# Attention stage of a token-merging block: raw-score search with three counts, dropped set added to transposed scores, values stationary in column groups

## What is computed

```python
qkv = (x_merge @ W_qkv).reshape(B, Mn, 3, NUM_HEADS, HEAD_DIM)
...
attn = jnp.einsum('bhqd,bhkd->bhqk', q, k) * SCALE
top_k = Mn // 8
kth = jax.lax.top_k(attn, top_k)[0][..., -1:]
attn = jnp.where(attn >= kth, attn, -jnp.inf)
attn = jax.nn.softmax(attn, axis=-1)
x_attn = jnp.einsum('bhqk,bhkd->bhqd', attn, v)
```

## Time and profile before

| | us |
|---|---|
| three runs: median (lowest to highest) | 15818.8 (15812.06 to 15821.48) |
| profiled execution, span | 16589.9 |
| attention in it, from its first score matmul to its last product | 3161 to 12898 |
| one step (one head), two consecutive ones | 72.85 and 71.58 |
| DVE / ACT / PE busy in 7000 to 7723 (10 steps) | 558.9 / 639.3 / 579.5 |

### The profile page before, as it was taken

One profiled execution on the slowest core, in us unless ns is written; L12 is line 12 of the kernel. 1 busy time (PEld: TensorE's weight loads), 2 busy tenths in 40 slices (PEclk: granted clock), 3 DMA queues, 4 the chain that ended last, 5 costly groups with the idle time before them and its releaser, 6 DMA issues. The chain is left out here.

```text
span 16589.9 us, 182616 instructions
## 1 busy us (share of the span) xinstructions
PE 10773.2 (65%) x53041; PEld 9450.6 (57%) x53041; DVE 10104.9 (61%) x21788; ACT 8925.2 (54%) x15905; POOL 2182.1 (13%) x2048
## 2 busy tenths in 40 slices
PE   4554776575888788878888866767678222229930
PEld 4454555375777777777777766767677222227720
DVE  7886344477777777777777777777777111111123
ACT  0000221486888888888888877878788010101100
POOL 2222111100000000000000000000000445440047
PEclk9999555555555555555555555555555555555555
DMA  2110000000000000000000000000000111111123
GB/s 71 37 31 22 19 21 19 16 5 4 6 6 6 6 6 6 5 5 6 6 6 6 6 4 5 5 6 6 4 6 4 30 34 30 34 26 32 32 47 58
DMA packets 624734, 282.98 MB, mean 17 GB/s; under 512 B 551011, under 2 KB 594595, under 8 KB 621061
## 3 DMA queue, kind: packets, MB, share of 16 engines
q1 hardware_dynamic: 563206, 222.50, 5.8%
q0 software_dynamic: 60928, 54.71, 1.6%
HBM read 167.59 MB, written 112.65 MB: 17 GB/s over the span
## 5 line engine op out<-in xcount | busy, mean ns | idle before, releaser
L971 PEld LDWEIGHTS a_psO<-a_v,a_pT 122*122 122x122 f32 x20736 | 4681.6, 329 | 0.0
L971 PE MATMUL a_psO<-a_v,a_pT 122*122 122x8 f32 x20736 | 4330.6, 333 | 0.0
L1047 ACT ACTIVATE a_signs<-a_e,a_te 122x1097 bf16<-122x1097 f32 x3456 | 4158.5, 1208 | 30.5
L961 PE MATMUL a_psT<-ident,a_p 122*122 122x122 f32 x10368 | 2918.3, 419 | 1789.9 <-ACT a_pT L1016 1342.0
L961 PEld LDWEIGHTS a_psT<-ident,a_p 122*122 122x122 f32 x10368 | 1955.5, 236 | 2138.9 <-issue 2138.7
L1016 ACT ACTIVATE a_pT<-a_psT 122x366 f32<-122x366 f32 x3456 | 1638.6, 474 | 388.7 <-PE a_psT L961 317.3
L1215 DVE TENSOR_REDUCE a_negmax<-a_psS 122x1 f32<-122x1097 f32 x1152 | 1493.7, 1297 | 572.7 <-PE a_psS L950 572.7
L1108 DVE SCALAR_TENSOR_TENSOR a_below<-a_e,a_te 122x1097 f32<-122x1097 f32 x1152 | 1553.0, 1348 | 210.7 <-remote 201.6
L1143 DVE SCALAR_TENSOR_TENSOR a_p<-a_e,a_theta 122x1098 f32<-122x1098 f32 x1152 | 1532.2, 1356 | 153.7 <-DVE a_flag L1184 135.0
L1054 ACT ACTIVATE a_e<-a_psS,a_negmax 122x1097 f32<-122x1097 f32 x1152 | 1384.5, 1202 | 290.9 <-DVE a_negmax L1215 290.8
L950 PE MATMUL a_psS<-a_k,a_q 72*122 72x512 bf16 (+1 forms) x3456 | 1325.7, 520 | 325.9 <-ACT a_e L1054 302.4
(11 more groups left out here) (343 smaller groups left out, 12886.9 us busy)
## 6 DMA issues: line engine op xcount, KB each, us to landing
r_bc<-pr SPq DMA_DIRECT2D x16, 1372.0 KB, 7.0
a_k<-kT SPq DMA_DIRECT2D x384, 51.5 KB
a_q<-qT SPq DMA_DIRECT2D x384, 51.5 KB
...
e_xg<-xbuf SPq DMA_DIRECT2D x160, 98.0 KB
ybuf<-e_yg SPq DMA_DIRECT2D x160, 98.0 KB
...
```

The source lines that it names most:

```text
L961: mm = pe.transpose(psT[:, j * QP:(j + 1) * QP], pr[t][:, kt * QP:(kt + 1) * QP], k.ident[0:QP, 0:QP])
L971: mm = pe.matmul(psO[:, 128 * u + t * HD:128 * u + (t + 1) * HD], pT[t % 2][:, kt, :], vh[u][:, kt * HD:(kt + 1) * HD], start=kt == 0, sto ...
L1047: act.activation(signs[t][:, :], ex[p][:, t, 0:MN], ACT.Sign, bias=te[p][:, t:t + 1], scale=-1.0, accum_out=sums[p][:, t:t + 1]).then_inc( ...
```

## The change

- **Scores stay raw.** DVE `evacuate` copies each score tile out of PSUM in two pieces (512 and 585 columns) with an accumulated maximum. `psS` is a single slot of 1536 columns; a piece is refilled as soon as it has been copied. There is no exp at this point.
- **Three counts.** ACT `count` counts at a first aim (mean + 1.185 deviations), at that moved by 0.9 of a slope step, and at that moved by another 0.5: 27 counts a head. The bracket and secant of `update` are gone; `move` is two small instructions, for tiles 0 to 4 and 5 to 8 apart.
- **Nearest 16.** DVE `window` writes min(score - te, sign) for the whole row, `nearest` takes the 8 largest of each of four quarters of it, `order` the 16 largest of these 32 (two MAX and a MATCH_REPLACE a tile). `search` picks the 137th; rows outside 16, or with more than 8 in a quarter, are marked, and marked tiles take the same kind of loop (`slow`) as before. The target count is 130 (TOPK - 7) instead of 133.
- **Dropped set.** `mask_tile` writes 1 where an element is under the threshold, as bf16 (`drops`), no accumulation. PE `fill` computes the transposed scores of 122 keys by 366 queries anew (`kt` stationary, `qt` moving, K = 74: two more rows carry minus the row maximum) and adds -32768 times the transposed `drops` in the same PSUM (three bf16 matmuls of 122 by 122, `drops` stationary). ACT `exponentials` then takes exp straight from PSUM for two blocks at a time (732 columns), 15 a head.
- **Values stationary.** PE `values`: v (122 by 32, with a column of ones for the row sum) is stationary, the 366 queries move (f32), and key block u writes to rows 32*(u mod 3) on of `psO`. ACT `take_out` copies 96 by 366 three times a head, and PE `turn_back` folds the three groups and turns the result back (9 f32 matmuls of 122 by 9). DVE `normalise` divides.
- **Row maximum.** PE turns it, DVE splits it into two bf16 parts (`split_peak`), SP writes it to DRAM and reads it back as two rows of `qt`. SP loads q and k twice a head (once for each orientation): 14 loads and a store in place of 7 loads.
- The pipeline is one step deeper (`old`: head s-3). A head's 15 slots are spread over 15 iterations of PE's step: iterations 0 to 9 belong to head s-2 (its slots 5 to 14), 10 to 14 to head s-1 (its slots 0 to 4).

In the diff, the removed functions are those printed above; lines that are only "..." stand for what is left out.

```diff
-AIM = TOPK - WIN // 2
-ROUNDS = 4
-Z_AIM = 1.15
+AIM = TOPK - 7
+Z_AIM = 1.185
...
-                                  SLOPE, None, ALU.mult).then_inc(free, 1)
+                                  -0.5 * SLOPE, None, ALU.mult).then_inc(free, 1)
...
+SUMK = PARTS * HP
+AUG = SUMK + 2
+CHUNKS = 3
+CT = QT // CHUNKS
+CW = CT * QP
+VC = 32
+NV = HD + 1
+PAIRS = [(0, 1), (2, 3), (4, 5), (6, 7), (8,)]
+PER = len(PAIRS)
+SLOTS = CHUNKS * PER
+RING = 3
+EDGES = [0, 275, 549, 823, MN]
+QUARTERS = len(EDGES) - 1
+HALF = 512
+FIRST_TILES = 5
+COUNTS = 3
+STEP = (0.9, 0.5)
+DROP = -32768.0
+LOWEST = -1.0e30
+EARLY = 3
+R_AT, PEAK_AT, FLAG_AT = 1104, 1280, 1408
+FLAG_SLOT = 9
+SCORE_AT = {9: (0, 1), 10: (2, 3), 11: (4, 5), 12: (6,), 13: (7,), 14: (8,)}
+assert CHUNKS * CT == QT and FLAG_AT + QT <= 1536
...
+        def slot(s, p, i):
+            return (s - 2, p, i + PER) if i < 2 * PER else (s - 1, 1 - p, i - 2 * PER)
...
+            def score(s, o, t, now, late):
                 n = QT * (s + 1) + t
                 if t == 0:
+                    pe.wait_ge(s_in[o], 16 * PARTS * (s + 3 - o))
+                wait(pe, evacuated, 2 * n - 1)
+                apart(pe, k)
+                q_ = qs[o][:, t * QP:(t + 1) * QP]
+                pe.matmul(psS[0:QP, 0:HALF], q_, ks[o][:, 0:HALF], start=True, stop=True).then_inc(scored, 1)
+                wait(pe, evacuated, 2 * n)
+                if t == 0 and now:
+                    wait(pe, peak_cut, s + 1)
+                if t == 0 and late:
+                    wait(pe, flagged, 2 * s)
+                apart(pe, k)
+                pe.matmul(psS[0:QP, HALF:2 * HALF], q_, ks[o][:, HALF:2 * HALF], start=True, stop=True)
+                pe.matmul(psS[0:QP, 2 * HALF:MN], q_, ks[o][:, 2 * HALF:MN], start=True, stop=True).then_inc(scored, 1)
+            def fill(h, q, j):
+                n = SLOTS * h + j
+                c, m = divmod(j, PER)
+                if j == 0:
+                    pe.wait_ge(t_in[q], 8 * (2 * PARTS + 2) * (h - q + 2))
+                if m == 0:
+                    wait(pe, masked, QT * h + CT * (c + 1))
                 wait(pe, exped, n - 1)
                 apart(pe, k)
+                for x, u in enumerate(PAIRS[m]):
+                    out = psT[(q + j) % 2]
+                    pe.matmul(out[:, x, 0:CW], kt[q][:, u * QP:(u + 1) * QP], qt[q][:, c * CW:(c + 1) * CW],
+                              start=True, stop=False)
+                    for t in range(CT):
+                        mm = pe.matmul(out[:, x, t * QP:(t + 1) * QP], drops[c * CT + t][:, u * QP:(u + 1) * QP],
+                                       weigh[:, :], start=False, stop=t == CT - 1)
+                mm.then_inc(filled, 1)
+            def values(h, q, j):
+                n = SLOTS * h + j
+                c, m = divmod(j, PER)
+                if m == 0:
+                    wait(pe, o_out, CHUNKS * h + c)
+                wait(pe, exped, n + 1)
                 apart(pe, k)
+                for x, u in enumerate(PAIRS[m]):
+                    g = u % CHUNKS
+                    mm = pe.matmul(psO[g * VC:(g + 1) * VC, 0:CW], vh[q][:, u, :], pT[j % RING][:, x, :],
+                                   start=u < CHUNKS, stop=u >= QT - CHUNKS)
+                mm.then_inc(valued, 1)
...
+                for t in range(QT):
+                    mm = pe.matmul(psS[0:QP, R_AT + t * NV:R_AT + (t + 1) * NV], oT[t // CT][:, t % CT * QP:(t % CT + 1) * QP],
+                                   fold[:, :], start=True, stop=True)
+                mm.then_inc(folded, 1)
+            def step(s, p, old, last, late, now, ahead):
                 o = 1 - p
+                for i in range(SLOTS):
+                    if old and i == 0:
+                        turn_back(s)
+                    if now and i == 2:
+                        wait(pe, peaked, s + 1)
+                        wait(pe, normed, s - 2)
                         apart(pe, k)
+                        pe.transpose(psS[0:QT, PEAK_AT:PEAK_AT + QP], peak[:, :], k.ident[0:QP, 0:QP]).then_inc(peak_turned, 1)
+                    if runs(i, last, late):
+                        values(*slot(s, p, i))
+                    if late and i == FLAG_SLOT:
+                        wait(pe, flagged, 2 * s - 1)
+                        apart(pe, k)
+                        pe.matmul(psS[0:1, FLAG_AT:FLAG_AT + QT], k.ones[0:QP, 0:1], bad[:, :], start=True,
                                   stop=True).then_inc(flag_sum, 1)
+                        fill(*slot(s, p, i + 1))
+                    if i != FLAG_SLOT - 1 and runs(i + 2, last, late):
+                        fill(*slot(s, p, i + 2))
+                    if ahead:
+                        for t in SCORE_AT.get(i, ()):
+                            score(s, o, t, now, late)
+            pe.wait_ge(k.started, 2)
             steps(pe, step)
         @block.scalar
...
+            def exponentials(h, q, j):
+                n = SLOTS * h + j
+                w = len(PAIRS[j % PER])
+                wait(act, valued, n - RING + 1)
+                wait(act, filled, n + 1)
+                act.activation(pT[j % RING][:, 0:w, :], psT[(q + j) % 2][:, 0:w, 0:CW], ACT.Exp).then_inc(exped, 1)
+            def take_out(h, c):
+                wait(act, folded, h)
+                wait(act, valued, SLOTS * h + PER * (c + 1))
+                act.activation(oT[c][:, :], psO[0:CHUNKS * VC, 0:CW], ACT.Copy).then_inc(o_out, 1)
+            def count(r, out, s_, t, at, total):
+                act.activation(out[:, :], s_[:, t, :], ACT.Sign, bias=at[:, t:t + 1], scale=-1.0,
+                               accum_out=total[:, t:t + 1]).then_inc(counted[r], 1)
+            def step(s, p, old, last, late, now, ahead):
                 o = 1 - p
+                i = 0
+                for n in range(COUNTS * QT):
+                    while i < SLOTS and i * COUNTS * QT <= n * SLOTS:
+                        if last and i % PER == 1:
+                            take_out(s - 2, i // PER)
+                        if runs(i, last, late):
+                            exponentials(*slot(s, p, i))
+                        i += 1
+                    r, t = n // QT, n % QT
+                    if r == 0 and now:
+                        if t in (0, FIRST_TILES):
+                            wait(act, aimed, 5 * s + (2 if t == 0 else 3))
+                        if t >= 2:
+                            wait(act, counted[1], QT * s + t - 1)
+                        count(1, junk[1][t % 2], sc[p], t, te[p], sums[1])
+                    if r == 1 and now:
+                        if t in (0, FIRST_TILES):
+                            wait(act, aimed, 5 * s + (4 if t == 0 else 5))
+                        wait(act, windowed, QT * (s - 1) + t + 1)
+                        count(2, signs[t], sc[p], t, te[p], last_sums[p])
+                    if r == 2 and ahead:
+                        if t == 0:
+                            wait(act, aimed, 5 * s + 6)
+                        wait(act, evacuated, 2 * (QT * (s + 1) + t + 1))
+                        if t >= 2:
+                            wait(act, counted[0], QT * (s + 1) + t - 1)
+                        count(0, junk[0][t % 2], sc[o], t, aim, sums[0])
             steps(act, step)
...
+            def move(s, p, r, half):
+                n = FIRST_TILES if half == 0 else QT
+                at = slice(0, n) if half == 0 else slice(FIRST_TILES, QT)
+                slope = k.stat[:, bass.ds(s, 1), 1, at].rearrange("p a t -> p (a t)")
+                wait(dve, counted[r], QT * s + n)
+                link.then(dve.scalar_tensor_tensor(out=moved[:, at], in0=sums[r][:, at], scalar=float(2 * AIM - MN),
+                                                   in1=slope, op0=ALU.add, op1=ALU.mult))
+                dve.scalar_tensor_tensor(out=te[p][:, at], in0=moved[:, at], scalar=STEP[r], in1=(te[p] if r else aim)[:, at],
+                                         op0=ALU.mult, op1=ALU.add).then_inc(aimed, 1)
+            def window(l, o, t):
+                wait(dve, counted[2], QT * l + t + 1)
+                dve.scalar_tensor_tensor(out=below[t % 3][:, :], in0=sc[o][:, t, :], scalar=te[o][:, t:t + 1],
+                                         in1=signs[t][:, :], op0=ALU.subtract, op1=ALU.min).then_inc(k.chain, 1)
+                link.n += 1
+            def nearest(t):
+                dve.wait_ge(k.chain, link.n - (t < QT - 1))
+                for g in range(QUARTERS):
+                    mx = dve.max(near[:, t, g, :], below[t % 3][:, EDGES[g]:EDGES[g + 1]])
+                    if g == 0:
+                        mx.then_inc(windowed, 1)
+                    else:
+                        link.after(mx, 9)
...
+            def mask_tile(l, o, t):
+                if t % CT == 0:
+                    wait(dve, filled, SLOTS * (l - 1) + PER * (t // CT + 1))
+                return dve.tensor_scalar(drops[t][:, 0:MN], sc[o][:, t, :], te[o][:, t:t + 1], kth[:, t:t + 1],
```

(40 more changed lines are left out.)

432 lines of the change are left out of this document (151 added, 281 removed).

## The result

The changed kernel takes 16356.33 us (median of 4 runs, 16354.0 to 16361.42) against 15818.17 us for the kernel before (4 runs): ratio 1.0341, 95% interval 1.0326 to 1.0355. It is 538 us slower. I had forecast 15520 us, in a range of 15000 to 16300: wrong in sign, and outside the range.

The account below looks back on a forecast made before the run. ACT's work and the four-trial ring between ACT and DVE bound the kernel (72.2 us a head). 128 x 62.7 + 1330 + 100 = 9456 us against 9737, rounded to 300 less: 15520 us, range 15000 to 16300.

Parts of the forecast that it names:

- Marked tiles: DVE's loop for rows the search fails on: 19 tiles at 70 us each, 1330 us instead of 420.
- Half B: Part of a step from the masks' release to DVE's last score copy: 26.0 us, between 23.0 and 32.1.
- my ring: Score tiles wait behind values and fills, these behind exps, these behind counts: tile 2 at 8.9 us, end 32.1 at 1.2 GHz.
- The clock: PE's dense stretches reach 2.4 GHz, gaps and scores take it back; hence a step of 62.7 us.
- half A: DVE's threshold search for head s-1, the part of a step before the masks' release: 36.4 us.
- Rival 1: PE at 1.2 GHz is the new bound: step 68.8 us, 500 us slower, 16320 us; chance 0.27.
- my 62.7: Forecast length in us of one step of the attention, with 26.0 us from the masks' release to the last copy.
- Rival 2: 2.4 GHz nearly throughout, or column groups side by side: step 59.7 us, 665 us faster, 15150 us; chance 0.25.
- three passes' time in place of four: PE's value passes of two key blocks overlap only in part: 2.4 us less after the masks' release at 1.2 GHz.
- Rival 3: DVE's masks run at one element a cycle, 1.25 us for 0.75: step 65, no change, 15820 us; chance 0.10.
- no wait for the DMAs of SP in `fill` 0: Extra loads and the store cost nothing; late ones would show at `fill` 0 of the next head.
- PE's ten slots and the turning back: PE's work beside DVE's search, before the masks' release: 35 us at 1.2 GHz, ten slots at 3.3.

Follow-up runs that it names:

- the three moves: Changed kernel with `take_out` one place earlier, score tiles 7 and 8 one slot earlier, score tile 0 ahead of the fills: 0.9584 of the kernel before (-659 us).
- experiment 8: Changed kernel with a pair's two value tiles in the same column group instead of two: 1.0338 of the kernel before (+550 us).

## Why the prediction was wrong, step by step

- **Marked tiles, the term that decides the sign.** I took 19 x 70 = 1330 us; it was 13, at 74 to 76 us each, some 960. The count from ordinary arithmetic was wrong on both sides, and not the same way (4 for 6, 19 for 13). This error hid a part of the other one: with the right count my forecast would have been 370 us lower still.
- **Half B, the term that failed.** I took 26.0 us, between my 23.0 for 2.4 GHz and 32.1 for 1.2; it was 34.2 (7046.5 to 7080.7), longer than the end to which I gave 0.27. What failed is the path through the queues. I left out `take_out`: one `psO` for three stretches, freed by ACT behind a count, 3.1 us in half B and 884 us in all. With it score tile 2 came 11.9 us behind the masks, for 8.9 in my ring at 1.2 GHz, and the later tiles 1.5 to 2.5 us late; a pair of values cost 1.44 us, not 2.5, which gave a part back. The waits that my ring did have, those for tiles 0, 7 and 8, I took as given; they were a matter of order as well. The first two fills were right (2.48 us for 2.4).
- **The clock.** I expected dense stretches of half A to reach 2.4 GHz: they did (0.81 us a pair at 7092.50). But half B ran at 1.2, a granted clock of 0.50, and the reason I gave for a value nearer to the fast end ("where PE is packed") does not hold there, since in half B PE waited for 8 of 34 us. By my own ring, 32.1 us at 1.2 GHz, this choice would be 6.1 of the missing 8.2 us. The runs show that the clock did not have to cost that: at the same 0.50 the three moves bring half B to 24.2 us, under my 26.0.
- **A wait that I put at nothing.** The 2.0 us a head at the head of a step, where the loop jumps back, are in no term of my sum, though the kernel before has them (202 us, before L1108). With them the step adds up: half A 36.1, the maximum 0.2, half B 34.2, this wait 2.0.
- **Rival 1** named the symptom: its sign was a wait of over 10 us a head for score tiles, and it was 18. Its clock in half B was right too. Its mechanism, PE's work as bound, is refuted for this kernel: with the same work and clock (0.57 and 0.58) the three moves take the step from 72.5 to 62.96 us, and only there is PE nearly full in half B. That this is within 0.3 of my 62.7 is luck: half B is 24.2 us there, for my 26.0, and the 2.0 us that I had not counted fill the gap. DVE's and ACT's work were priced right (PE's too high); the order in which the queues release one another was not. Its step of 68.8 was too low by 3.7.
- **Rival 2.** My bound "three passes' time in place of four" was wrong: four passes in two groups take 1.44 us, as one group needs 2.62 (experiment 8), a ratio of 1.8. The Trainium skill ("TensorE: Matmul & The Clock Gate", "Measured speedup vs the span model") has 2.38 for three groups; the trace agrees in kind, with two at a time. The step gained nothing by it: with one group (experiment 8) the kernel is only 12 us longer, at a higher clock.
- **Rival 3** is out: a mask lasts 0.851 us and starts 0.76 after the last.
- **What held.** ACT 5609 / 128 = 43.8 us a head for 42.6; half A 36.1 us of work for 36.4; DVE's long waits at tiles 7, 8 and after the flag, though not the 4.49 us at tile 2; no wait for the DMAs of SP in `fill` 0. DVE's work in half B was 17.1 us; my terms 12.6 + 4.6 make 17.2, and I wrote 17.5. PE's ten slots and the turning back make 36.9 us by my prices, and I wrote 35. Neither changes the forecast.
- **The sum.** With 72.5 for 62.7 and 957 for 1330, 128 x 9.8 - 373 = +881 us on 15520: 16401, against 16356 measured.
